# Aggregations: GpSimd's wait for seven of the preceding eight gathers stands only where its loop of four steps turns over

## The reference

```python
hW = h @ W + b                       # 6250 x 64
e  = leaky_relu(s[row, head] + d[col, head])
ex = exp(e - m[row]);  alpha = ex / den[row]
out[row] += alpha[:, None] * hW[col] # over all 200000 edges
```

## Time and profile before

| | |
|---|---|
| profiled execution | 7063.9 us, span 7062.1 us |
| median of three runs | 7060.26 us |
| first aggregation, 495 to 2737 us | 2242 us |
| second aggregation, 3582 to 5875 us | 2293 us |
| sort and first table, experts and second table, tail and dense layer | 495, 845 and 1187 us |
| POOL busy in the span | 3469.1 us (49%) |
| DVE busy in the span | 4389.3 us (62%) |
| PE busy in the span | 5095.9 us (72%) |

### The profile page before, as it was taken

How to read it: one execution, slowest core, us unless ns; L and a number is a source line. 1 busy time by engine, 2 the same in 40 slices (tenths; PEclk the granted TensorE clock), 3 DMA queues, 4 the chain that set the end, 5 groups by cost and what they waited for, 6 DMA issues and landing times. The chain is left out here.

```text
span 7062.1 us, 90296 instructions
## 1 busy us (share of the span) xinstructions
PE 5095.9 (72%) x21196; PEld 3660.6 (52%) x21197; DVE 4389.3 (62%) x8953; ACT 1783.8 (25%) x4856; POOL 3469.1 (49%) x3669
## 2 busy tenths in 40 slices
PE   1446666666666664699766666667777777999999
PEld 1445555555555552466534444445555555666666
DVE  8987777777777778722566655556666667333333
ACT  7322222222222222222310000001111113433332
POOL 0126767666767766144146666666666664000000
PEclk8668888888888886799878887877777777999999
DMA  1022222222222222322444444444444444000001
GB/s 55 22 44 51 52 52 52 52 51 52 52 52 52 52 51 58 116 64 64 145 135 124 125 123 123 123 124 130 130 132 132 132 131 114 5 5 4 9 4 36
DMA packets 380644, 534.45 MB, mean 76 GB/s; under 512 B 119264, under 2 KB 240119, under 8 KB 380407
## 3 DMA queue, kind: packets, MB, share of 16 engines
q0 software_dynamic: 139648, 299.92, 17.8%
q1 hardware_dynamic: 240886, 233.29, 11.2%
HBM read 475.96 MB, written 56.96 MB: 75 GB/s over the span
## 5 line engine op out<-in xcount | busy, mean ns | idle before, releaser
L876 POOL DMA_INDIRECT got<-table,st_idx x3232 | 3092.9, 957 | 1453.5 <-issue 1004.8
L952 PE MATMUL ps_sum<-weighted,hot 128*128 128x260 f32 x6464 | 1861.2, 447 | 143.2 <-DVE acc L1024 139.0
L952 PEld LDWEIGHTS ps_sum<-weighted,hot 128*128 128x128 f32 x6464 | 1403.1, 229 | 563.0 <-DVE acc L1024 228.8
L1024 DVE TENSOR_TENSOR acc<-acc,ps_sum 128x260 f32 x1664 | 707.1, 425 | 890.3 <-PE ps_sum L952 750.0
L937 PE MATMUL ps_score<-score_split,hot_t 128*128 x3232 | 250.1, 188 | 1294.7 <-DVE z L1004 1267.5
L937 PEld LDWEIGHTS ps_score<-score_split,hot_t 128*128 128x128 bf16 x3232 | 196.8, 103 | 1471.7 <-issue 1456.7
L1016 DVE TENSOR_TENSOR weighted<-got,ps_weight 128x2048 f32<-128x2048 f32 x404 | 921.5, 2281 | 4.3 <-ACT weighted L912 0.8
L909 ACT ACTIVATE ps_weight<-z 128x32 f32<-128x32 f32 x404 | 81.2, 201 | 2969.8 <-DVE z L1004 2969.8
L3058 DVE SCALAR_TENSOR_TENSOR x_res<-ps_yf,comb,x_res 128x256 f32 x392 | 189.7, 484 | 638.0 <-PE ps_yf L2966 638.0
L975 DVE TENSOR_TENSOR hot<-ps_score,row_loc 128x1024 f32<-128x1024 f32 x404 | 492.1, 1218 | 3.5
L993 DVE TENSOR_REDUCE row_score<-ps_score 128x64 f32<-128x192 f32 (+1 forms) x404 | 163.3, 404 | 520.3 <-DMA got<-table,st_idx 518.9
(11 more groups left out here) (533 smaller groups left out, 7558.3 us busy)
## 6 DMA issues: line engine op xcount, KB each, us to landing
spread<-row_list SPq DMA_DIRECT2D x404, 256.0 KB
got<-table,st_idx POOLq DMA_INDIRECT x3232, 2.8
gate_xin<-ball_rows SPq DMA_DIRECT2D x98, 128.0 KB
got_y_e<-y_rows SPq DMA_DIRECT2D x10, 896.0 KB
table<-row_e SPq DMA_DIRECT2D x50, 130.0 KB, 2.6
ball_rows<-xt SPq DMA_DIRECT2D x10, 640.0 KB, 4.7
mix_xin<-ball_rows SPq DMA_DIRECT2D x49, 128.0 KB
xn_rows<-xs_m SPq DMA_DIRECT2D x49, 128.0 KB, 1.7
```

Of the source, the lines that this page charges most:

```text
L876: pool.indirect_dma_start(got[:, r, k, :], None, table, bass.IndirectOffsetOnAxis(ap=st_idx[:, r, k:k + 1], axis=0))\
L952: last = nc.tensor.matmul(ps_g[:, p % 2, 0:AW], hot[:, r % 2, k, :], weighted[:, r % 2, k, :], start=(k == n * p), stop=(k == n * p + n - 1))
L1024: nc.vector.tensor_tensor(acc[:, ds(b * AW, AW)], acc[:, ds(b * AW, AW)], ps_g[:, p % 2, 0:AW], ALU.add).then_inc(added, 1)
```

## The change

The wait on `gathered` is kept for r = 0 alone, in all turns but the first, and dropped for r = 1, 2 and 3, in the first turn too. The count waited for at r = 0 is the one before: all seven first gathers of r = 3 of the turn before, since (turn - 1) * 112 + 112 is turn * 112. Nothing else differs; the waits on `idx_staged` and `scaled` stay in every step.

```diff
@@ -868,9 +868,8 @@
                 pool.wait_ge(idx_staged, j + 1)
                 if not first:
                     pool.wait_ge(scaled, j - (STEP_RING - 1))
-                if not first or r > 0:
-                    t, q = (turn, r - 1) if r else (turn - 1, STEP_RING - 1)
-                    pool.wait_ge(gathered[q], t * (16 * (KT - 1)) + 16 * (KT - 1))
+                if r == 0 and not first:
+                    pool.wait_ge(gathered[STEP_RING - 1], turn * (16 * (KT - 1)))
                 pool.nop(nofuse=True)
                 for k in range(KT):
                     pool.indirect_dma_start(got[:, r, k, :], None, table,
```

## The result

The changed kernel takes 6719.95 us (median of 4 runs, 6714.86 to 6722.13) against 7060.53 for the kernel before (4 runs, 7059.98 to 7061.63): a ratio of 0.9516, 95% interval 0.9500 to 0.9533.

The account below looks back on a forecast made before the run. POOL, held at step boundaries by waits for gathers to land, was taken as the bound in most stretches. Savings of 121 + 87 + 45 = 253 us off 7063.9 gave 6811, or 6807 us against the runs; range 6760 to 6885 us.

Parts of the forecast that it names:

- the two POOL terms: Gather waits removed at 151 boundaries per aggregation: POOL saves 121 us in the first, 174 us (87 each half) in the second.
- The choice of 0.305 over 0.72: Gap at a step boundary without the wait: taken as 0.305 us, with 0.72 us, the shortest boundary then, kept for the range.
- what was to show it: Trace signs: 0.30 us gaps at three of four steps, POOL idle near 560 us, shorter steps, less DVE waiting for gathers.
- In the second half DVE's 10.57 is longer than POOL's 10.44, so DVE becomes the bound: Second half of the second aggregation: us per step; at most 72.6 us of DVE's waiting could go, 45 us taken.
- my rival of 0.15: POOL stays the bound throughout, as PE's clock rises and DVE's step falls below 10.44 us: 295 us saved, 6765 us; chance 0.15.
- which come with no wait and stay: 18 gaps of 1.67 us inside steps of the first aggregation, one every 88 gathers, 25 us above the rest, expected unchanged.
- DVE and PE: Rival: DVE and PE bound all of the second aggregation, so 187 us are saved in all, 6873 us; chance 0.14.
- the 0.72-us boundary: Rival: boundaries without the wait keep 0.72 us because register-computed waits are not free; 155 us saved, 6905 us; chance 0.08.
- The slower one: Rival: gathers stand behind VectorE instructions on the shared SBUF port, 356 us more in POOL's queue, 7163 us; chance 0.06.

Follow-up runs that it names:

- the fills: Dummy matmuls a step in the second aggregation: ten on the kernel before, 7064.22 us; on the kernel without gather waits, ten 6622.94 us, twenty 6629.42 us.

## Why the prediction was right, and where it failed

The main part held. POOL's waiting for landing was the bound, three boundaries of four fell to 0.30 us, and the two POOL terms came: 51 x 0.762 + 50 x 0.747 + 50 x 0.839 = 118 us in the first aggregation (121 forecast) and 51 x 1.191 + 50 x 1.036 + 50 x 1.224 = 174 us in the second (87 + 87 potential). The choice of 0.305 over 0.72 was right, and the run with the waits two steps back shows why: a wait that is met costs nothing here.

Of what was to show it, POOL's idle time in the first aggregation came to 534.5 us (near 560 expected), and VectorE's waiting to 184.1 us there (near 175). POOL's steps became shorter than expected, 10.29 us (10.5) and 10.33 us (10.4 to 10.8). The time forecast was 87 us too high, for three reasons.

- **The step that failed**: "In the second half DVE's 10.57 is longer than POOL's 10.44, so DVE becomes the bound". A fixed step would have let 72.6 of POOL's 87 us through; I took 45, because pairs at the lower clock were longer still. The step fell to 10.24 us instead, so POOL (10.33 us) stayed the bound and all 87 arrived: 42 us. This was my rival of 0.15; its 6765 us were still 45 too many, for the two reasons that follow. The earlier trace rows had the dependence on the clock; what I did not see is that the clock would move with the change. That the clock shortens the step is shown by the fills, with no wait on the gathers altered. That a faster pace raises the clock is not shown; it rests on a comparison of kernels: the pairs' mean was 0.742 and 0.751 at 12.5 and 11.3 us a step, and 0.770 to 0.793 in the seven kernels without fill at 10.1 to 10.4 us. Among those seven the clock does not go in the order of the pace (0.782 at 10.15 us, 0.790 at 10.33).
- **"which come with no wait and stay"**, of the 18 gaps of 1.67 us: wrong. They stand only behind a wait that held. 14 of 18 went in each aggregation, 2 x 14 x 1.37 = 38 us. A gap that names no releaser is not one without a cause. Where the period of 88 gathers comes from stays open; no run varied it.
- **Small ones**: the wait at r = 0 became shorter, 50 x (0.151 + 0.116) = 13 us, gathers in the first aggregation took 0.956 instead of 0.965 us, 14 us in sum, and those of the second 5 us more in sum, so 9 us in all.

Together 292 + 38 + 13 + 9 = 352 us, which the two windows have within 2 us (159 + 191 = 350). The last gather starts 350 us earlier, but the last exponents only 343.8: VectorE trails POOL by more (16 us where it was 10), and 342 reach the end of the profiled execution.

The other rivals fell: DVE and PE did not bind the second aggregation, and the 0.72-us boundary does not exist without a wait. The slower one, VectorE's port: without any pause a gather beside a one-hot is still longer, as in the kernel without waits:

```profile
5004.84 0.48 DVE L979 TENSOR_SCALAR hot_t<-spread,lane 128x1024 bf16<-128x1024 bf16 x1
...
5005.00 1.14 POOL L873 DMA_INDIRECT got<-table,st_idx  x1 [0.30 <-issue]
```

The mean is 954 and 949 ns even there, 965 and 949 before: meetings did not become more. The Trainium skill describes a lock in "SBUF — State Buffer", section "Who interferes with whom"; the 1.14 us agree with it, but it decides nothing here.

## What to carry to other kernels

Ask of a wait whether it is met when the engine comes to it: moved two steps back, nearly the same number of waits cost nothing. When an off-path engine's step is to become the bound, ask what that step was made of while it waited: here a part of it was waiting for TensorE, whose clock was higher once the change was in. And a periodic gap without a named releaser may belong to the wait ahead of it; list where it stands before keeping it in the sum.

## What the runs showed of the hardware

- Two indirect gathers of 128 rows follow each other with 0.30 us between, and 0.95 us each, for 1616 in a row, and their landing stays at a median of 2.5 and 2.8 us without any wait on it.
- Where a gather was awaited that had not landed, the next one started 0.74 to 0.86 us after the landing, at all 402 boundaries of the kernel that waits for all eight.
- Every 88th gather has 1.67 us ahead of it instead of 0.30, if the gather before it had a wait that held: 18 times an aggregation with a wait at every step, 4 times with one at r = 0, 5 times with one at r = 1, and never where no wait held.
- Ten more matmuls a step in idle time raised TensorE's granted clock over 46 pairs of steps from 0.751 to 0.808 (kernel before) and from 0.773 to 0.848 (without waits), twenty to 0.879; the same 63 matmuls of a pair took 17.69 us at 0.69 and 15.29 us at 0.85.
